# Sequence attention on one core: normaliser reciprocals in a compact form, LayerNorm scaling on ScalarE, weight split on GpSimd, batches written out

## The reference

```
x = x + masked grouped attention(layernorm(x), ctx)     # stage a
x = x + ternary FFN(layernorm(x))                       # stage b
x = x + sequence attention(layernorm(x), ctx, ctx)      # stage c
x = x + gated FFN(layernorm(x))                         # stage d
```

```
qk  = einsum('bhdq,bhdl->bhql', qh, kh) / sqrt(32)      # 8 heads, 512 x 512 each
ret = einsum('bhql,bhdl->bhdq', softmax(qk), vh)
x   = x + gamma * ret
```

## Time and profile before

| | us |
|---|---|
| median of 3 runs | 1853.65 (1852.92 to 1854.41) |
| profiled execution, own time | 1850.29 |
| span of the profiled execution | 1848.5 |
| stage c, first load issued to last store issued | 975.4 to 1318.0 |

### The profile page before, as it was taken

The page is one execution under the profiler, slowest core; times in us unless marked ns, Lnnn a source line. Parts: engine busy times, 40 slices in busy tenths (PEclk is TensorE's granted clock), DMA queues, the critical chain, the costliest instruction groups (busy, mean ns, idle before and its releaser), DMA issues. The chain is left out here.

```text
span 1848.5 us, 25537 instructions
## 1 busy us (share of the span) xinstructions
PE 1489.4 (81%) x9033; PEld 657.7 (36%) x9106; DVE 959.9 (52%) x1526; ACT 678.6 (37%) x1212; POOL 404.6 (22%) x502
## 2 busy tenths in 40 slices
PE   3568878877787747867672898899599999999998
PEld 2334534444343213333330122222144444444443
DVE  6544744646646358788853788888332032131220
ACT  2153444444434424544440566666322021121120
POOL 4210101101100046666642233342200000000000
PEclk8678988889888968888885899999799999999999
DMA  5524254253442121111113556453300100100100
GB/s 137 91 87 107 81 142 87 96 127 81 122 97 72 58 66 34 45 40 41 44 35 120 164 180 217 150 194 117 124 1 0 69 1 1 68 0 0 46 0 23
DMA packets 91704, 146.29 MB, mean 79 GB/s; under 512 B 7624, under 2 KB 48136, under 8 KB 90064
## 3 DMA queue, kind: packets, MB, share of 16 engines
q1 hardware_dynamic: 78816, 119.93, 22.9%
q10 hardware_dynamic: 12800, 25.17, 4.3%
HBM read 114.23 MB, written 30.83 MB: 78 GB/s over the span
## 5 line engine op out<-in xcount | busy, mean ns | idle before, releaser
L488 DVE TENSOR_REDUCE a_negmax<-a_psX 128x4 f32<-128x1024 f32 x128 | 149.8, 1216 | 170.9 <-PE a_psX L682 170.3
L1349 DVE TENSOR_REDUCE c_negmax<-c_psA 128x1 f32<-128x512 f32 x256 | 163.9, 673 | 60.4 <-PE c_psA L1420 58.2
L373 ACT ACTIVATE a_probs<-a_psB 128x512 f32<-128x512 f32 x256 | 138.5, 593 | 145.6 <-PE a_psB L692 145.5
L1653 PE MATMUL d_psGU<-d_zt_lo,last_w_hi 128*128 128x512 bf16 x501 | 189.9, 379 | 2.2 <-DVE d_zt_lo L1607 1.7
L1653 PE MATMUL d_psGU<-d_zt_hi,last_w_hi 128*128 128x512 bf16 x502 | 190.3, 379 | 0.6
L1653 PE MATMUL d_psGU<-d_zt_hi,last_w_lo 128*128 128x512 bf16 x501 | 189.9, 379 | 0.6
L1576 ACT ACTIVATE d_silu<-d_psGU 128x512 f32<-128x512 f32 x64 | 38.2, 597 | 378.2 <-PE d_psGU L1653 378.2
L692 PE MATMUL a_psB<-a_qs,a_ks 115*128 115x256 bf16 x512 | 138.7, 401 | 45.7 <-ACT a_probs L373 40.2
L1295 ACT ACTIVATE c_probs<-c_psB 128x512 f32<-128x512 f32 x256 | 142.2, 595 | 90.8 <-PE c_psB L1433 88.6
L1618 DVE TENSOR_TENSOR d_h<-d_psGU,d_silu 128x512 f32<-128x512 f32 x64 | 44.2, 691 | 236.4 <-PE d_psGU L1653 236.4
L1420 PE MATMUL c_psA<-c_ks,c_qs 96*128 96x512 bf16 x256 | 105.1, 412 | 50.6 <-DMA c_qs<-q_scr 29.1
(11 more groups left out here) (207 smaller groups left out, 2641.9 us busy)
## 6 DMA issues: line engine op xcount, KB each, us to landing
a_tern_stage<-in_w ACTq DMA_DIRECT2D x32, 768.0 KB, 7.5
c_weight_stage<-in_w_last SPq DMA_DIRECT2D x8, 1536.0 KB, 8.7
a_ks<-k_scr SPq DMA_DIRECT2D x24, 256.0 KB
a_qs<-q_scr SPq DMA_DIRECT2D x24, 256.0 KB
c_ks<-k_scr SPq DMA_DIRECT2D x48, 128.0 KB, 2.6
c_qs<-q_scr SPq DMA_DIRECT2D x48, 128.0 KB, 3.0
a_xz<-in_x SPq DMA_DIRECT2D x8, 512.0 KB, 18.5
a_ctx<-in_ctx_t SPq DMA_DIRECT2D x8, 512.0 KB, 12.7
```

The lines of the kernel that those rows point to most:

```text
L373: act.activation(pr[:, e % 4, :, jj * P:(jj + 1) * P].rearrange("p r (a i) -> p a r i", a=2), B[:, u % 2, :].rearrange("p (a r i) -> p a r ...
L488: v.tensor_reduce(negm[:, u, :], X[:, 2 * (u % 2):2 * (u % 2) + 2, :].rearrange("p a (j k) -> p (a j) k", k=SEQ), AX.X, ALU.max, negate=Tr ...
L1349: v.tensor_reduce(negm[:, u:u + 1], A[:, u % 2, :], AX.X, ALU.max, negate=True)\
L1653: last = pe.matmul(GU[:, 2 * up + i % 2, :], wgu[wh][:, k, o:o + P], zt[zh][:, k, :], start=(k == 0 and j == 0), stop=(k == DC - 1 and j = ...
```

## The change

Five edits, all in stage c:

1. ScalarE copies a quad's outputs and sums (PSUM, 128 x 1024) to SBUF. One row of sums per head goes to DRAM (4 x 512), comes back as 128 x 16, VectorE takes the reciprocal of that, and it goes to DRAM and comes back broadcast to 128 x 512. All four transfers are issued by ScalarE. `finish` reads SBUF only.
2. `finish` and the reciprocals have new places: `finish(b-1, 0)` at k = 2 and the reciprocal of (b-1, 1) at k = 3 of quad 0, `finish(b-1, 1)` at k = 2 and the reciprocal of (b, 0) at k = 3 of quad 1. `update(b-1, 0)` and `update(b-1, 1)` on GpSimd follow them. Before, `finish(b, 0)` ran in batch b and `finish(b-1, 1)` in the first quad of batch b.
3. The LayerNorm scaling moves from VectorE to ScalarE (Identity with scale and bias); GpSimd makes the bias in two small operations. `inputs(m)` on VectorE moves up to k = 1, on ScalarE z_hi moves from after step 5 to after step 6.
4. The high half of the weights is a cast on GpSimd.
5. The batch loop is written out; every `hold` becomes a plain wait. On SyncE, `shift_in(n, 0)` goes ahead of `store(b-1)`.

The diff, cut to its core (replacements of `hold` by `need` with the same value are left out, as are the new declarations of `nmr`, `os_sb`, `s16`, `r16` and the DRAM scratch `s1_scr`, `r1_scr`):

```diff
         def run(engine, first, attend):
             first()
-            attend(0, 0, 1, 2)
...
-            attend(BATCH - 1, 1, None, None)
+            for b in range(BATCH):
+                attend(b, b % 2, b + 1 if b + 1 < BATCH else None, b + 2 if b + 2 < BATCH else None)
...
# sync, attend
                 if n is not None:
                     shift_out(n, 0)
+                if n is not None:
+                    shift_in(n, 1 - par, 0)
                 if not begins(b):
                     store(b - 1)
-                if n is not None:
-                    shift_in(n, 1 - par, 0)
...
# gpsimd
             def inputs(n):
...
+                for t in range(ST):
+                    g.tensor_scalar(nmr[:, t:t + 1], mv[:, t, 0:1], rstd[:, t:t + 1], -1.0, ALU.mult, ALU.mult)\
+                        .then_inc(s["rstd_done"], 1)
...
             def attend(b, par, n, m):
...
                 if not begins(b):
-                    update(b - 1, 1)
-                if m is not None:
-                    low(m)
+                    update(b - 1, 0)
                 for k in range(WP):
+                    if k == 1 and not begins(b):
+                        update(b - 1, 1)
+                    if k == 1 and m is not None:
+                        low(m)
...
+                    pool.wait_ge(s["stage_loaded"], (b + 1) * DMA)
+                    g.tensor_copy(wf_hi, stage[:, k * WU // WP:(k + 1) * WU // WP]).then_inc(s["stage_split"], 1)
...
-                update(b, 0)
             run(pool, first, attend)
+            update(BATCH - 1, 0)
             update(BATCH - 1, 1)
...
# scalar
+            def scale(n):
+                act.wait_ge(s["rstd_done"], ST * (n + 1))
+                act.wait_ge(s["xz_loaded"], (n + 1) * DMA)
+                need(act, s["z_lo"], n)
+                for t in range(ST):
+                    act.activation(z[:, t, :], xz[:, t, :], ACT.Identity, scale=rstd[:, t:t + 1], bias=nmr[:, t:t + 1])\
+                        .then_inc(s["z_ready"], 1)
...
+            def results(b, quad, stage_of):
+                k = 2 * b + quad
+                if stage_of == 0:
+                    act.wait_ge(s["pv_done"], EG * b + QT * (quad + 1))
+                    need(act, s["ret_done"], k - 1)
+                    need(act, s["sums_moved"], 2 * k * DMA)
+                    act.activation(os_sb[:, quad].rearrange("p a n -> p (a n)"), OS[:, quad].rearrange("p a n -> p (a n)"), ACT.Copy)\
+                        .then_inc(s["os_copied"], 1)
+                    act.wait_ge(s["os_copied"], k + 1)
+                    act.dma_start(io["s1_scr"], os_sb[0:P:32, quad, 1, :]).then_inc(s["sums_moved"], DMA)
+                elif stage_of == 1:
+                    act.wait_ge(s["sums_moved"], (2 * k + 1) * DMA)
+                    need(act, s["recip_done"], k)
+                    act.dma_start(s16[:], io["s1_scr"].rearrange("j (a q) -> (j a) q", q=D // 32)).then_inc(s["sums_moved"], DMA)
+                elif stage_of == 2:
+                    act.wait_ge(s["recip_done"], k + 1)
+                    need(act, s["recip_moved"], 2 * k * DMA)
+                    act.dma_start(io["r1_scr"].rearrange("j (a q) -> (j a) q", q=D // 32), r16[:]).then_inc(s["recip_moved"], DMA)
+                else:
+                    act.wait_ge(s["recip_moved"], (2 * k + 1) * DMA)
+                    need(act, s["ret_done"], k)
+                    act.dma_start(rec[:], io["r1_scr"].rearrange("j (o q) -> j o q", o=1).broadcast_to([4, 32, D]))\
+                        .then_inc(s["recip_moved"], DMA)
...
             def attend(b, par, n, m):
...
+                    if e == 1 and not begins(b):
+                        results(b - 1, 0, 3)
+                        results(b - 1, 1, 0)
+                    if e in (2, 4, 5) and not begins(b):
+                        results(b - 1, 1, (e + 1) // 2)
+                    if e in (5, 6):
+                        results(b, 0, e - 5)
                     if e == 2 and m is not None:
                         context(m)
-                    if e == QT + 1 and m is not None:
+                    if e == 4 and m is not None:
+                        scale(m)
+                    if e == QT + 2 and m is not None:
                         inputs(m)
-                    if e in (3, 6, 7):
-                        weights(b, (3, 6, 7).index(e))
                 if n is not None:
                     exponentials(n, 0)
+                results(b, 0, 2)
             run(act, first, attend)
+            results(BATCH - 1, 0, 3)
+            for stage_of in range(4):
+                results(BATCH - 1, 1, stage_of)
...
# vector
+            def reciprocals(b, quad):
+                k = 2 * b + quad
+                dve.wait_ge(s["sums_moved"], 2 * (k + 1) * DMA)
+                need(dve, s["recip_moved"], (2 * k - 1) * DMA)
+                v.reciprocal(r16[:], s16[:]).then_inc(s["recip_done"], 1)
             def finish(b, quad):
...
+                dve.wait_ge(s["recip_moved"], 2 * (k + 1) * DMA)
+                need(dve, s["x_updated"], k)
+                v.scalar_tensor_tensor(out=ret[:], in0=os_sb[:, quad, 0, :], scalar=gamma[:], in1=rec[:],
                                        op0=ALU.mult, op1=ALU.mult).then_inc(s["ret_done"], 1)
             def first():
                 dve.wait_ge(s["gamma_loaded"], DMA)
                 inputs(0)
-                scale(0)
+                inputs(1)
...
             def attend(b, par, n, m):
                 for quad in range(2):
                     for k in range(QT):
                         if n is not None:
                             maxima(n, quad, range(4 * k, 4 * k + 2))
...
+                        if quad == 0 and k == 2 and not begins(b):
+                            finish(b - 1, 0)
+                        if quad == 0 and k == 3 and not begins(b):
+                            reciprocals(b - 1, 1)
+                        if quad == 1 and k == 2 and not begins(b):
+                            finish(b - 1, 1)
+                        if quad == 1 and k == 3:
+                            reciprocals(b, 0)
                         if n is not None:
                             maxima(n, quad, range(4 * k + 2, 4 * k + 4))
...
             run(dve, first, attend)
+            finish(BATCH - 1, 0)
+            reciprocals(BATCH - 1, 1)
             finish(BATCH - 1, 1)
# tensor: O and S become the two halves of OS; outputs wait for os_copied in place of ret_done
```

More of the change, by code:

```diff
@@ L1168, in store @@
             def store(b):
[L1169 removed]
+                need(sp, s["x_updated"], ST * (b + 1))
                 sp.dma_start(x_out[bass.ds(b * SEQ, SEQ), :].rearrange("(t p) d -> p t d", p=P), xr[:])\
@@ L1378, in first @@
                     split_max(0, quad)
-                    if quad == 0:
-                        inputs(1)
-                        scale(1)
             def attend(b, par, n, m):
                 for quad in range(2):
-                    last = (b, 0) if quad else (b - 1, 1)
-                    ends = quad == 1 or not begins(b)
                     for k in range(QT):
@@ L1390, in attend @@
                             maxima(n, quad, range(4 * k, 4 * k + 2))
-                        if ends and k < 3:
-                            reciprocals(*last, k)
-                        elif ends:
-                            finish(*last)
+                        if quad == 0 and k == 2 and not begins(b):
[6 more added lines that the diff above has]
+                            reciprocals(b, 0)
                         if n is not None:
                             maxima(n, quad, range(4 * k + 2, 4 * k + 4))
-                        if ends and k == 0:
-                            reciprocals(*last, 3)
-                        if quad == 0 and k == 2 and m is not None:
+                        if quad == 0 and k == 1 and m is not None:
                             inputs(m)
@@ L1402, in attend @@
                         split_max(n, quad)
-                    if quad == 0 and m is not None:
-                        scale(m)
             run(dve, first, attend)
-            for k in range(QT):
-                reciprocals(BATCH - 1, 1, k)
+            finish(BATCH - 1, 0)
+            reciprocals(BATCH - 1, 1)
             finish(BATCH - 1, 1)
@@ L1448, in sums @@
                 for j in range(4):
-                    last = pe.matmul(S[32 * j:32 * j + 32, e // QT, :], keep["ones"][:, 0:32], pr[:, e % 2, j, :],
+                    last = pe.matmul(OS[32 * j:32 * j + 32, e // QT, 1, :], keep["ones"][:, 0:32], pr[:, e % 2, j, :],
                                      start=(kt == 0), stop=(kt == QT - 1))
```

100 lines of the change are left out of this document (43 added, 57 removed).

## The result

| | before | after | forecast |
|---|---|---|---|
| median, us | 1853.68 | 1958.42 (1956.66 to 1960.04) | 1902 (1882 to 1926) |
| ratio, 95% interval | | 1.0565 (1.0547 to 1.0583) | 1.026 |
| span of the profiled execution | 1848.5 | 1954.9 | |
| stage c, first load to last store | 342.6 | 448.6 | |

The change makes the kernel 105 us slower. The sign and the main mechanism were forecast, the size was not: 1958 lies 32 us above the range. The first line of the page has every engine's share down but GpSimd's, most of all because the span is longer. VectorE's own busy time falls by 44 us, which is the relief that the change bought.

A forecast was written before the change was run, and what follows sets the result against it. TensorE was taken to set stage c's pace, with small holes. 1850.3 - 5.4 (start) + 47.5 (five stalled batches) + 0 + 6.7 (tail) = 1899.1; the runs' median lies 3.4 higher, so 1902 us, range 1882 to 1926.

The forecast's parts named there:

- New place of `finish(b-1, 1)`: Stage c, step 6: late finish delays store, xr and stacks; TensorE stands 9.8 us at five batches' first maximum.
- The period: Time per stalled batch of stage c: 46.5 us against 37.0, +47.5 over five; bounds 42.6 and 51.5.
- Behind step 2 the c_hi cast waits for its transfer as before: ScalarE in stage c: the cast's wait unchanged, with a hole of 0.85 us in step 2.
- The clock: After the stall at a batch's first maximum: 3 us at half speed, counted as 1.2 us per period.
- Rival B: ScalarE held by its own transfers between steps 1 and 2: six times 3 us, 1920 in all; chance 0.15.
- VectorE relieved: Stage c: four 0.94 us reciprocals per quad become one of 0.2; holes of some 1.5 us in steps 1 and 5 go.
- `finish` blocked behind GpSimd: VectorE, step 2: finish with two SBUF inputs could block up to 2.1 us, six up to 12; counted as none.
- `split_max`: VectorE operation that GpSimd's cast pieces could lengthen by up to 2 us without the stall; counted as nothing.
- Start: Start of stage c: inputs(1) and its scaling come before the first maximum, -5.4 us.
- Batches 0, 6, 7: Stage c batches without the chain's stall period: no change, each 0 +-2 us.
- Tail: From last matmul to last store: copy, four transfers, reciprocal, finish, update take 12.3 us, +6.7; bounds +4 to +12.
- Rivals A and C: A: chain doesn't reach TensorE, 1846, chance 0.08 with its neighbourhood; C: faster transfers shorten the stall, 1889, chance 0.12.

The follow-up runs named there:

- x_late_direct: Changed kernel without the four DRAM transfers: VectorE takes 128 x 128 reciprocals from ScalarE's SBUF copy; late finish, update and store stay; 1903.94 us.
- x_compact_best: Changed kernel with sums' write before broadcast, finish(b-1, 0) later, low(m) before update(b-1, 1), halves_out and stack before store, xr load later; 1915.86 us.

## Why the prediction was wrong in size

- **New place of `finish(b-1, 1)`: right.** Every link is met: 3.0 us into step 6 (3.1 forecast), store issued at 5.1 (5.25), store to xr 2.76 (2.96), xr to stacks 7.07 (6.9), first maximum at 20.5 (20.4). TensorE waits 8.3 to 8.8 us five times (9.8); what is missing stands just ahead, as the wait of the transpose for `split_max` (below).
- **The period: 46.5 forecast, 54.7 measured.** From first maximum to step 6 (1119.69 to 1153.97) it is 34.3 us where I had 26.1, and five times 8.2 are 41 of the 57 us that the sum is short. The step that failed is the one on ScalarE: "Behind step 2 the c_hi cast waits for its transfer as before", a hole of 0.85. It is 7.0 in batch 2. That is 6.1 us; in batches 1 to 5 the hole sums to 36.0. The clock is the second term: I counted one fall at 1.2 us, and there are two per batch. In this stretch TensorE is busy 26.9 us, 3.4 more than 22.3 clean and 1.2 for the clock. Against them stand the other holes, 1.8 forecast and 0.35 found. 6.1 + 3.4 - 1.45 is 8.1. The stated upper bound, 51.5, was passed too: it allowed for 4 us of holes.
- **Rival B: the right mechanism, 0.15, at a third of its size.** It was 18 us; x_late_direct puts the path through DRAM at 54.5. (Its own terms, 2.4 and about 1, make 3.4 a batch, not 3.) I priced the write at the slowest of L1161's landings, 6.4, and took its own queue as a point against the wait. The queue was the cause: the 256 KB broadcast stood in it 1.7 us ahead, and the write took up to 12.8 us from issue until the load behind it could go. The edit's part 1 puts both into one queue, and the prediction listed the four issues without asking which of them stands behind which.
- **The late place by itself.** x_late_direct has neither the transfers nor the relief. Its period of 48.5 is the forecast's 46.5 with the 1.5 us of reciprocal holes left in, within half a microsecond, though the clock and the small holes in it were not taken apart. That its total, 1903.94, is close to 1902 is partly chance: it lacks the tail's transfers.
- **VectorE relieved: right, and of little worth.** The reciprocals sum to 3.9 us (0.24 each; 0.2 taken). Even all of them left out win only about 10 us. `finish` blocked behind GpSimd, weighed at up to 12 us and counted at nothing, cost nothing: none of the 16 `finish` took over 0.752 us after the change.
- **`split_max`: named, then counted as nothing.** I wrote that GpSimd's pieces could block it were the stall not there. They do with it there: the cast of 128 x 16 takes 0.88 on average and up to 2.04, and step 0's transpose waits 1.0 to 1.4 us behind it in batches 2 to 6, as the row of 1165.41 shows. It costs nothing of its own: the wait lies inside the 20.5 us of the chain and makes the stall behind it shorter by as much.
- **Start: right in place** (-5.1; -5.4). That it reaches the end in full isn't shown: alone it gave 1.9 us by batch 7.
- **Batches 0, 6, 7: 0 +- 2 each forecast; batches 0 and 6 together +3.6 (92.1 less five times 17.7), batch 7 +7.8.** In batch 7 ScalarE waits 4.16 us for the write of sums at 1384.44, again behind a broadcast (1375.75), and the clock averages 0.89 there. x_late_direct, without the transfers, has 22.4 in this place, as before.
- **Tail: +6.7 forecast, +11.2.** The working was right but for two of its transfers. Timelines of ScalarE's queue and of VectorE:

```profile
1404.92 0.54 ACTq L1331 DMA_DIRECT2D c_recip<-r_scr  x1
1406.64 0.51 ACTq L1319 DMA_DIRECT2D s_scr<-c_out_sums  x1
1411.42 0.32 ACTq L1323 DMA_DIRECT2D c_sums<-s_scr  x1
1413.24 0.33 ACTq L1327 DMA_DIRECT2D r_scr<-c_sums_recip  x1
1414.66 0.54 ACTq L1331 DMA_DIRECT2D c_recip<-r_scr  x1
1419.65 0.75 DVE L1411 SCALAR_TENSOR_TENSOR c_ret<-c_out_sums,c_gamma,c_recip 128x512 f32<-128x512 f32 x1 [6.45 <-DMA c_recip<-r_scr]
```

The write takes 4.8 us, again behind a broadcast (2.1 taken), and the broadcast 5.0 with nothing else in flight (2.7 taken); the other two, 1.5 and 1.4, were overpriced. The four make 12.7 where the forecast had 9.0.
- **Rivals A and C: refuted.** The chain reaches TensorE, and it isn't faster with the other queues quiet.

The sum once more, with the measured parts: 1850.3 - 5.1 + 92.1 + 7.8 + 11.2 = 1956.3, against 1956.7 for the profiled execution's time (span 1954.9 and 1.8 around it).

## What to carry to other kernels

Before an engine's compute queue gets a small transfer on which it later waits, list what stands ahead of it in the same queue: 8 KB behind 256 KB cost some 7 us per batch here, and swapping two lines gave back a third of the loss. Before a cheap operation is made cheaper by way of DRAM, run the kernel with the operation left out; here it showed a prize of about 10 us for a path that, with its late places, cost 114. And when an operation moves later, follow its result through every queue in which its store stands ahead of something else.

## What the runs showed of the hardware that was not expected

- A load of 256 KB that repeats four rows over 128 partitions takes 5.0 us alone. The windows of its last stretch (columns as above) show a DMA share near a quarter (0.22, 0.25 and 0.20 in the three microseconds from 1416), and at most 96 GB/s:

```profile
1417.00:1418.00 1.00, 0.00 (x0) 0.00 (x0) 0.00 (x0) 0.00 (x0) 0.00 (x0) 0.50 0.25 96
```

The share is that of 4 of the 16 DMA engines, and the load reads four rows, its outermost dimension; no run here changes their number, so that this is the reason isn't shown. The Trainium skill, DMA: Bandwidth & Descriptors, section Anatomy of one DMA, has a fit for transfers that GpSimd issues, which would make it an estimated 2.6 us. ScalarE issues this one, and the measurement is almost twice that.
- VectorE's `finish` with two SBUF inputs takes 0.74 us where GpSimd is quiet. In x_compact_best it began 0.32 after a GpSimd operation of 2.13 and took 2.36:

```profile
1150.44 2.36 DVE L1417 SCALAR_TENSOR_TENSOR c_ret<-c_out_sums,c_gamma,c_recip 128x512 f32<-128x512 f32 x1
```

That agrees with the rule of the Trainium skill, SBUF — State Buffer, section Who interferes with whom, which the prediction weighed. The cast in `split_max`, with one SBUF input, was held too: 2.04 us in place of 0.17, beside a GpSimd operation that began 0.12 before it and ended at 1164.34, where the cast ended at 1164.37. The timeline of both engines after the change:

```profile
1162.21 2.13 POOL L1266 TENSOR_TENSOR last_w_lo<-c_weight_stage,last_w_hi 128x1024 bf16<-128x1024 f32 x1
1162.33 2.04 DVE L1397 CAST c_max_split<-c_negmax 128x16 bf16<-128x16 f32 x1
```

- A second queue beside a burst lengthens above all the last load of the burst. The medians of the eight loads went from 4.6 to 4.9 us for v, from 5.3 to 5.7 for xz and from 6.1 to 8.5 for ctx. In batch 2 the three took 5.5, 6.0 and 6.7 before, 6.8, 8.1 and 9.4 after, and 9.8, 10.6 and 11.3 in x_chain, where SyncE's own queue held more ahead of them as well.
